# Triangle and mark in one weight; the target plan and its edge fetches inside the sort loop

## The reference, cut to what matters

```python
edge_index = jnp.stack([src, dst])
h = jnp.maximum(_layernorm(x, axis=-1), 0.0)
x = x + _L0_gnn_ref(h, src, dst, ...)      # segment sums over dst
h = jnp.maximum(_layernorm(x, axis=-1), 0.0)
x = x + _L1_gnn_ref(h, ..., edge_index, edge_type_64, 0)   # three hops, segment sums over src
```

## Time and profile before

| what | us |
|---|---|
| median of 3 runs | 9552.52 (9550.24 to 9559.58) |
| the profiled execution | 9554.53 |
| its span | 9552.7 |
| sort loop, first to last slot reduction | 63.42 to 634.20 |
| last run store issued | 643.74 |
| target edges being decoded from | 672.38 |
| source edges being decoded from | 700.93 |

### The profile page before, as it was taken

The page is one execution under the profiler, slowest core; times in us unless marked ns, Lnnn a source line. Parts: engine busy times, 40 slices in busy tenths (PEclk is TensorE's granted clock), DMA queues, the critical chain, the costliest instruction groups (busy, mean ns, idle before and its releaser), DMA issues.

```text
span 9552.7 us, 271679 instructions
## 1 busy us (share of the span) xinstructions
PE 7999.1 (84%) x62097; PEld 6935.3 (73%) x62097; DVE 7758.0 (81%) x33664; ACT 7498.1 (78%) x24462; POOL 6812.7 (71%) x7069
## 2 busy tenths in 40 slices
PE   8977777777776888888887888888887888888887
PEld 7866666666665777777776777777776777777776
DVE  8989999999997777777777777777777777777776
ACT  6739999999986777777777777777777777777776
POOL 2347777777775777777776777777776777777776
PEclk9989999999998999999998999999998999999999
DMA  2014444444444555555555555555555555555555
GB/s 55 5 35 108 108 108 110 108 108 108 108 113 132 157 161 156 159 157 158 161 155 167 157 158 159 157 161 156 159 159 163 161 156 159 158 158 161 156 160 147
DMA packets 1127114, 1309.11 MB, mean 137 GB/s; under 512 B 446660, under 2 KB 840730, under 8 KB 1126716
## 3 DMA queue, kind: packets, MB, share of 16 engines
q1 hardware_dynamic: 896038, 843.26, 28.7%
q0 software_dynamic: 229264, 460.98, 19.0%
q10 hardware_dynamic: 1670, 3.16, 0.1%
HBM read 1041.61 MB, written 261.38 MB: 136 GB/s over the span
## 4 chain that ended last, share of the span: by engine, by line
PE 35%; DMA 21%; issue 15%; DVE 12%; POOL 10%; ACT 4%; SPq 1%; DVEq 1%; POOLq 0%; ACTq 0%
PE bank L782 27%; DMA agg<-agg_d,arena 18%; POOL agg L744 10%; PE bank L959 3%; PE bank L944 3%; PE bank L912 2%; DVE agg L1689 2%; DVE agg L1679 2%; DVE arena L1788 2%; ACT arena L1100 2%; DMA agg<-feat_d,arena 1%; ACT arena L1180 1%; DVE arena L1765 1%; DVE arena L1669 1%; DVE arena L1647 1%
## 5 line engine op out<-in xcount | busy, mean ns | idle before, releaser
L744 POOL DMA_INDIRECT agg<-agg_d,arena x5124 | 4871.6, 951 | 1687.1 <-issue 1380.6
L1788 DVE TENSOR_TENSOR arena<-agg,bank 128x256 f32<-128x256 f32 x2562 | 1079.8, 421 | 1404.7 <-DMA agg<-agg_d,arena 1184.5
L782 PE MATMUL bank<-arena 128*128 128x129 f32 x10248 | 1763.1, 295 | 305.1 <-ACT arena L1180 297.8
L744 POOL DMA_INDIRECT agg<-feat_d,arena x1708 | 1619.5, 948 | 532.1 <-issue 418.5
L782 PEld LDWEIGHTS bank<-arena 128*128 128x128 f32 x10248 | 1378.9, 195 | 434.5 <-issue 409.4
L1176 ACT ACTIVATE arena<-arena 128x1 f32<-128x1 f32 x2562 | 755.4, 295 | 1158.1 <-DVE arena L1653 1121.8
L782 PE MATMUL bank<-tmp,wide 128*128 128x256 f32 x5124 | 1577.9, 391 | 6.4 <-DMA wide<-left_d 6.4
L782 PE MATMUL bank<-tmp,kw_s 128*128 128x256 f32 x5124 | 1567.3, 388 | 0.1
L959 PE MATMUL bank<-ident,arena 128*128 128x128 f32 x5124 | 1027.3, 283 | 509.6 <-DVE arena L1788 506.6
L959 PEld LDWEIGHTS bank<-ident,arena 128*128 128x128 f32 x5124 | 695.4, 144 | 932.4 <-DVE arena L1788 709.3
L1171 ACT ACTIVATE arena<-agg,arena 128x256 f32<-128x256 f32 x2562 | 1342.4, 524 | 17.6 <-DVE arena L1781 12.1
(11 more groups left out here) (251 smaller groups left out, 16728.2 us busy)
## 6 DMA issues: line engine op xcount, KB each, us to landing
state_d<-arena SPq DMA_DIRECT2D x488, 455.0 KB
arena<-key_d SPq DMA_DIRECT2D x489, 448.0 KB
arena<-type_d SPq DMA_DIRECT2D x367, 448.0 KB
wide<-left_d SPq DMA_DIRECT2D x2562, 64.0 KB
agg<-agg_d,arena POOLq DMA_INDIRECT x5124
agg<-feat_d,arena POOLq DMA_INDIRECT x1708
arena<-er_d SPq DMA_DIRECT2D x854, 1.0 KB
arena<-peers SPq DMA_DIRECT2D x489, 7.0 KB
```

The source lines that it names most:

```text
L744: nc.gpsimd.indirect_dma_start(out=rows_r[:, k % R, c, 0:width], out_offset=None, in_=table, in_offset=bass.IndirectOffsetOnAxis(ap=peer_r ...
L782: return nc.tensor.matmul(out, lhsT, rhs, start=start, stop=stop)
L1788: V.tensor_tensor(val_r[:, j % R, :, 0:F], rows_r[:, j % R, :, 0:F], bank[0][:, 0:G].rearrange("p (c f) -> p c f", c=2), ALU.mult).then_in ...
```

## The change

1. `mark16` becomes triangle plus mark (one more VectorE add at the start), and the separate matmul on `before16` goes: one matmul fewer in each half of the ranks. The run sizes are counted on the six pair sums and the last one-hot: 7 matmuls instead of 13.
2. The plan of the targets moves to chunks 66 to 101, the totals to 62, the table matmuls to 78 to 90.
3. The 7 fetches of target edges move into the loop: POOL issues one behind the stores of chunks 104, 106 ... 116, the first after waits for `packed_stored`, `windows_in[0]` and `feat_stored`. Should the fallback be taken, they are repeated in it.
4. POOL signals `order_settled` behind its branch. VectorE decodes the targets after `plan_member(1)`, when the fetches have landed and `order_settled` is there; the source tables and lists follow. TensorE's turns of the target peers wait for the 8 table copies, since they share banks with the source tables. The fetches by source no longer stand behind those by target.

```diff
-SIGNS_AT, TOTALS_AT = 12, 68
+SIGNS_AT, TOTALS_AT = 12, 62
+FETCH_AT = 104
-TABLES_AT = (84, 88, 92, 96)
+TABLES_AT = (78, 82, 86, 90)
...
             for n in range(CHUNKS):
...
+                if n == FETCH_AT:
+                    pool.wait_ge(packed_stored, 16)
+                    pool.wait_ge(windows_in[0], 16)
+                    pool.wait_ge(feat_stored, 32)
+                if FETCH_AT <= n < FETCH_AT + 2 * R and (n - FETCH_AT) % 2 == 0:
+                    fetch(0, (n - FETCH_AT) // 2, resorted_in)
             pool.wait_ge(run_stored, 16 * CHUNKS)
...
+            pool.wait_ge(resorted_in, 16 * R)
             pool.wait_ge(order_known, 1)
...
             with pool.Else():
                 apart(pool)
-
-            for s in range(2):
-                if s == 0:
-                    pool.wait_ge(windows_in[0], 16)
-                    pool.wait_ge(feat_stored, 32)
-                else:
...
+            pool.sem_inc(order_settled, 1)
+
+            pool.wait_ge(tails_known, 1)
...
+            pool.wait_ge(windows_in[1], 16)
+            pool.wait_ge(decoded, 1)
+            pool.wait_ge(tails_stored, 16)
+            apart(pool)
+            for k in range(R):
+                fetch(1, k, resorted_in)
...
-                    mm(to, before16[:], block_hot[:, h, lo:hi, :], True, False)
-                    mm(to, mark16[:], block_hot[:, h, lo:hi, :], False, False)
+                    mm(to, mark16[:], block_hot[:, h, lo:hi, :], True, False)
...
-                for c in range(SC):
-                    last = mm(bank[6][0:NB, 0:1], block_hot[:, h, c, :], ones16[:, 0:1], c == 0, c == SC - 1)
+                for m in range(COUPLES):
+                    mm(bank[6][0:NB, 0:1], couple[:, h, m, :], ones16[:, 0:1], m == 0, False)
+                last = mm(bank[6][0:NB, 0:1], block_hot[:, h, SC - 1, :], ones16[:, 0:1], False, True)
...
                         pe.wait_ge(decoded, s + 1)
+                        pe.wait_ge(table_copied, 8)
...
-            V.tensor_scalar(mark16[:], colid[:], rowid[:, 0:1], MARK, ALU.is_equal, ALU.mult)
+            do(V.tensor_scalar(mark16[:], colid[:], rowid[:, 0:1], MARK, ALU.is_equal, ALU.mult))
+            V.tensor_tensor(mark16[:], mark16[:], before16[:], ALU.add)
...
-                if n == 72:
+                if n == 66:
                     plan_windows(0)
-                elif n == 77:
+                elif n == 71:
                     plan_rows(0)
-                elif n == 82:
+                elif n == 76:
                     dve.wait_ge(feat_stored, 32)
                     plan_member(0)
-                elif n in (86, 90, 94, 98):
-                    plan_table(0, (n - 86) // 4)
+                elif n in (80, 84, 88, 92):
+                    plan_table(0, (n - 80) // 4)
+                elif n == 95:
+                    plan_lists(0)
+                elif n == 97:
+                    plan_keep(0)
+                elif n == 99:
+                    plan_limits(0)
                 elif n == 101:
-                    plan_lists(0)
-                elif n == 104:
-                    plan_keep(0)
-                elif n == 108:
-                    plan_limits(0)
-                elif n == 112:
                     plan_targets(0)
...
             plan_rows(1)
-            plan_member(1)
-            for i in range(4):
-                plan_table(1, i)
-            plan_lists(1)
...
+                    dve.wait_ge(order_settled, 1)
...
+            plan_member(1)
+            decode(0)
+            for i in range(4):
+                plan_table(1, i)
+            plan_lists(1)
...
-            decode(0)
             plan_keep(1)
             plan_limits(1)
             plan_targets(1)
```

More of the change, by code:

```diff
@@ L361, in gnn_kernel @@
         order_known = sem("order_known")
+        order_settled = sem("order_settled")
         windows_stored = [sem(f"windows_stored{i}") for i in range(2)]
@@ L597, in _, with fetch @@
             pool.wait_ge(prefilled, 32)
+            def fetch(s, k, done):
+                nc.gpsimd.indirect_dma_start(
+                    out=s_packed[:, k * G:(k + 1) * G], out_offset=None, in_=sorted_edges[s].rearrange("(w e) o -> w (e o)", e=G),
+                    in_offset=bass.IndirectOffsetOnAxis(ap=window_of[s][:, k:k + 1], axis=0)).then_inc(done, 16)
             for n in range(CHUNKS):
@@ L708, in _ @@
                 scatter_all(1, lambda c: other_f.bitcast(I32)[:, c:c + 1], 16 * SC * PAIRS)
+                for k in range(R):
+                    fetch(0, k, scattered[0])
+                pool.wait_ge(scattered[0], 2 * 16 * SC * PAIRS + 16 * R)
                 apart(pool)
@@ L711, in _ @@
                 apart(pool)
-            for s in range(2):
-                if s == 0:
-                    pool.wait_ge(windows_in[0], 16)
-                    pool.wait_ge(feat_stored, 32)
-                else:
[L718 to L729, removed]
+            pool.sem_inc(order_settled, 1)
+            pool.wait_ge(tails_known, 1)
+            nc.gpsimd.indirect_dma_start(
+                out=sorted_edges[1], out_offset=bass.IndirectOffsetOnAxis(ap=tail_at[:, 0:1], axis=0),
+                in_=filler[:], in_offset=None).then_inc(tails_stored, 16)
+            pool.wait_ge(windows_in[1], 16)
+            pool.wait_ge(decoded, 1)
+            pool.wait_ge(tails_stored, 16)
+            apart(pool)
+            for k in range(R):
+                fetch(1, k, resorted_in)
             def gather(layer):
```

## The result

The changed kernel takes 9536.3 us (median of 20 runs, 9527.3 to 9545.5), the kernel before beside it 9550.2 (20 runs): a ratio of 0.9985, 95% interval 0.9978 to 0.9991. It is 14 us faster where 41 were forecast, and 4 us above the range. The profiled executions have spans of 9535.6 and 9552.7 us; that of before lay a little above its median, which is why spans differ by 17 and medians by 14.

The account below looks back on a forecast made before the run. TensorE was taken to bound the sort loop, by under half a microsecond a chunk over VectorE. Loop -33.8 + 3 = -30.8, tail -10.4, sum -41.2: 9554.5 to 9513.3 us, predicted 9512, range 9501 to 9532.

Parts of the forecast that it names:

- The weights: Sort loop: fewer mark and size matmuls cut TensorE's plain chunk period from 4.50 to 4.06 us, with VectorE limiting the gain.
- (a): Sort loop: three engines within 0.05 us do not mesh, plain period 4.20 us; costs 14 us, total 9526; chance 0.14.
- (d): Sort loop: dropped matmuls were under something else, TensorE is not shortened, only the tail gains; total 9542; chance 0.05.
- The moved plan: Chunks 65 to 101: whole target plan there takes 167.0 us, each piece counting in full, closer packing costing nothing more.
- Chunks 0 to 15: Loop's first zone, with the packing work, bound by VectorE: 79.8 us before, 79.3 after.
- The fetches in the loop: Seven target fetches behind stores 104 to 116: 7.3 us of POOL against 8.1 a pair; cost 3 us, bounds 0 and 7.
- 3 us of lead in the four run buffers: Loop's run stores: lead subtracted from a 10 us worst-case fetch delay, giving the upper bound of 7 us.
- Rival (b): Loop fetches not hidden: each pair loses 0.3 + 1.7 + 0.3 us, 16 us for seven; total 9525; chance 0.12.
- rival (c): Store chain becomes the bound: chunks 52 to 123 lose 40 us, late landings behind fetches 38; total 9587; chance 0.04.
- The rule of the Trainium skill that was weighed: Loop: two-input VectorE instructions contend with GpSimd ones reading SBUF, so fetches come off worse there than in the quiet tail.
- The tail: Behind the loop: first source fetch about 24 us after the last store's landing, source decoding about 45 (55 before); -10.4 us.
- The sum: Whole kernel up to source decoding: loop -30.8 us and tail -10.4 us make -41.2 us.

Follow-up runs that it names:

- The narrow fetches: Changed kernel with each loop fetch taking 32 edges a row instead of 256, from another place; 9919.8 us, 1.0387 of the kernel before.
- the fastest kernel: Changed kernel with seven target fetches behind the last run store, plan in small portions, target decoding after source tables and lists; 9520.6 us, 0.9967 of the kernel before.

## Why the forecast was wrong, step by step

**The weights: right.** 4.05 computed, 4.06 taken, 4.07 measured. Chunks 16 to 38 took 92.94 (93.5), 39 to 51 59.68 (59.7), 52 to 64 52.52 (52.4). Rivals (a) and (d) are out.

**The moved plan: the sum was nearly right, its condition was not.** Chunks 65 to 101 took 174.2 us, 7.2 more than 167.0. In portions they took 167.75, at a clock of 1.00, and 1.1 us more in the chunks before. One piece had been read too short: keep lengthens its chunk in the kernel before by 549.38 - 541.78 less 4.03 = 3.6 us, not 2.6. The forecast said that packing the pieces closer costs nothing, "since the sum counts", and that the granted clock would still be 1.00. The first holds for VectorE. TensorE, though, now waits up to 3.1 us in one go at a piece, and its clock fell. The longest such wait before was 2.0 us, at a clock of 1.00. That it takes both the shorter matmuls and the long pieces is shown from both sides: the same pieces with the old matmuls keep 1.00, and so do the new matmuls with the pieces cut up. The length of the single wait does not decide it: with the weights alone the gathers are slow behind a wait of 1.54 us, and with the old matmuls they are not behind one of 2.26. Nor is it the move: with the weights alone the pieces stand in their old chunks. So this loss belongs to the shorter matmuls beside pieces that were there already, which the forecast put at nothing. In packed form the early plan saved nothing: chunks 52 to 122 take 310.7 us with the weights alone, 310.2 with the packed early plan and no fetches, 306.1 in portions.

**Chunks 0 to 15** took 82.1 us, not 79.3, at a clock of 0.89. Every kernel with the new weights took 80.5 to 82.4 there, the two without 79.8 and 78.9. The same instructions took 80.5 us at a clock of 0.95 or 0.96 in two of these traces and 82.1 to 82.4 at 0.89 or 0.90 in four, and 80.6 and 81.4 at 0.90 in the other two. I did not test what in that stretch would restore it; that the cause is the clock is argued, not shown.

**"The fetches in the loop" is the step that failed.** It had bounds of 0 and 7 us and took 3; measured are 14.8 (11.6 in the loop, 3.2 in the stores that trail it). It set 7.3 us of POOL's time for a pair against 8.1; the pair shown takes 10.7. Half of the difference is issue: the two stores' and the fetch's come to 2.54 + 1.84 + 2.00 us with 0.30 twice, 7.0 us, where the forecast had 5.3. The other half is idle time. The forecast let "the first store's landing" lie under the fetch, which is right, and took the second store's at the usual 2.0. But the fetch's transfer, 122 rows of 256 edges or 125 KB, is ahead of that store, and the store lands 1.7 us later. The next store waits for this landing.

The "3 us of lead in the four run buffers" was there, but it is no discount. Store 107 is issued 3.0 us later than in the kernel with the fetches behind the loop while no slot reduction up to chunk 111 is later by more than 0.01 us; store 114 is 10.0 us later, and the reduction of chunk 119, which follows the first cursor that needs it, 7.0. So VectorE is spared 3 us and waits for the rest, 11.0 us in all. The path behind the loop, however, starts from the last store's landing, and there the 3.2 us come back. Nor does the chain win much back by itself: it asks for 2.0 us of waiting and, in these traces, mostly 1.6 to 2.3 us of issue, out of 4.07 us a chunk. Even with the weights alone and no fetch, the last store is issued 10.6 us behind the last reduction, not the 9.5 of the kernel before.

Rival (b) had the place and the size (16 us for seven fetches, at 2.3 each), but charged it all to issue time. The narrow fetches have the same issues and cost 5.9 us. The first half of rival (c) did not come true: chunks 52 to 64 run at 4.04 us and VectorE does not wait for landings there. Its second half, that a store behind a fetch lands late, did, with 1.7 us instead of the 3.4 that it charged.

The rule of the Trainium skill that was weighed (SBUF — State Buffer, Who interferes with whom) would have made the fetches' issue the cost. The seven fetches in the loop take 1.69 to 2.93 us, 2.03 in the mean, and those in the quiet tail 1.67 to 2.08, 1.77 in the mean; so if the rule is at work on them, it shows by 0.3 us a fetch, a small part of the 2.1. The Trainium skill (DMA: Bandwidth & Descriptors, Two DMAs through the same engine are not ordered) bears on what was found: it says that within one queue of one DMA engine descriptors start in order, though they are pipelined. The late landing of the store behind a fetch, 1.7 us, agrees with that, and it is gone when the fetch is narrow.

**The tail: right in sum, in part by luck.** Target decoding came 8.35 us after the landing (8.4), source decoding 45.55 (44.6 to 45). In between, errors nearly cancelled: the small store of the windows took 3.90 us (2.5 to 4.1 had been allowed for it and the reload together, 5.5 were measured; the last section has what stood beside it), so the first source fetch came at 26.7 instead of 24; and the last landing took 6.34, not 7.4, with the fetches themselves 12.5 instead of 13.1.

**The sum.** Source decoding was forecast 41.2 us earlier and came 18.7 earlier. The 22.5 between them: chunks 102 to 122 +11.2 less the 3 allowed for, chunks 65 to 101 +7.2, chunks 0 to 15 +2.8, other zones -0.5, the start of the loop -0.6, the stores trailing the loop +4.4 (13.9 against 9.5 us), the tail +0.9 or so. Read by cause, 11.8 of the 22.5 are the fetches beyond their 3 us (14.8 measured), and 10.0 are the two zones in which the clock was lower. The portions give back 5.4 of these 10.0; they take away the long waits and the lower clock together, so the share of the clock alone is not shown.

## What to carry to other kernels

When the bounding engine is made faster, count the slack of every chain again at the new period, the chain of a DMA's landing above all, before work is moved into the loop: here POOL's time was set against the new period, but with a store's issue and landing as they were without a fetch. A DMA put into a chain costs not only its issue but also the later landing of whatever stands behind it in its queue. Buffers that let an engine run ahead hide such a delay from that engine; they do not take it off a path that ends on the last store. Side work of one engine that makes TensorE wait should be cut into portions, and the granted clock read stretch by stretch after the change.

## What was not expected of the hardware

- TensorE's granted clock fell in a stretch in which it is 93% busy (162.78 of 174.22 us), where it had waited 2.5 us at a time, and the 26 gather matmuls behind it took 4.04 instead of 2.39 us. With the weights alone a wait of 1.54 us was followed by 3.87.
- Seven or four fetches, behind every second chunk or every fourth: 2.1 and 2.05 us each. Spacing bought nothing in sum.
- POOL's branch costs 3.6 us although its fallback is not taken (3.7 in the kernel before, 645.92 to 649.65). In the fastest kernel the last fetch's issue ends at 629.34, its landing, for which POOL waits, fits 633.76 (6.1 us after the issue began, as in the earlier trace rows), and the signal behind the branch comes at 637.33:

```profile
629.34 4.42 issue
633.76 0.50 POOLq L715
...
637.33 0.03 POOLq L729
```

- The same small store of the window list landed after 3.90 us in the changed kernel, and after 1.25 us in the kernel before. The traces sort by what else is under way. In the five kernels that decode the targets before the source lists, SP has begun the 427 KB store of the decoded keys some 6 us earlier (650.69 in the changed kernel), and the small store takes 3.9 to 4.0 us; in the five others that large store comes later, and it takes 1.2 to 1.7 us. No run moved the large store alone.
